# Reading the row of column numbers from PSUM in the one-hot matrices of a graph network's sum passes

## What is computed

```
h = relu(layernorm(x)); x = x + spline_conv(h, edge_attr)       # batch norm and ELU inside
h = relu(layernorm(x)); x = x + attention_conv(h)               # softmax over the edges of a node
h = relu(layernorm(x)); x = x + gcn3(h)
h = relu(layernorm(x)); x = x + sage(h)

gcn3:  three times  h = relu( sum over edges of (h @ W)[src] * norm  + self term + b )
sage:  concat(segment_sum(h[src], dst) / deg, h) @ W.T + b
segment_sum(src_rows, dst, num_segments=N)
```

## Time and profile before

| | |
|---|---|
| median of 3 runs | 13193.13 us (13179.23 to 13198.88) |
| profiled execution, time | 13194.91 us |
| profiled execution, span of the profile | 13193.0 us |
| PE busy | 7957.6 us (60%) |
| POOL busy | 8307.1 us (63%) |
| DVE busy | 5160.7 us (39%) |
| ACT busy | 1792.7 us (14%) |
| granted tensor clock, mean | 0.750 of full speed |

### The profile page before, as it was taken

The page is one execution under the profiler, slowest core; times in us unless marked ns, Lnnn a source line. Parts: engine busy times, 40 slices in busy tenths (PEclk is TensorE's granted clock), DMA queues, the critical chain, the costliest instruction groups (busy, mean ns, idle before and its releaser), DMA issues.

```text
span 13193.0 us, 199759 instructions
## 1 busy us (share of the span) xinstructions
PE 7957.6 (60%) x44286; PEld 5757.4 (44%) x44287; DVE 5160.7 (39%) x12670; ACT 1792.7 (14%) x4699; POOL 8307.1 (63%) x7522
## 2 busy tenths in 40 slices
PE   5878888888646666676666345534545345524445
PEld 5777888888534555555555111121112111101112
DVE  6545555555633333333334222232223222242223
ACT  0000011111123333333443000000000000000000
POOL 5788888777566666665442666646665566646664
PEclk9888899999767777788887566656666566656666
DMA  6111111111132222222221333323332232323332
GB/s 250 18 16 15 16 16 16 15 15 15 4 69 64 61 61 59 59 60 61 62 56 32 76 85 82 85 50 82 85 82 61 74 85 79 85 55 83 85 85 67
DMA packets 533179, 800.90 MB, mean 61 GB/s; under 512 B 319934, under 2 KB 329453, under 8 KB 532837
## 3 DMA queue, kind: packets, MB, share of 16 engines
q0 software_dynamic: 311952, 330.95, 14.0%
q1 hardware_dynamic: 218485, 466.48, 11.1%
q10 hardware_dynamic: 2400, 0.53, 0.0%
HBM read 700.08 MB, written 97.36 MB: 60 GB/s over the span
## 4 chain that ended last, share of the span: by engine, by line
issue 21%; DVEq 18%; PE 11%; another core or an unknown queue 10%; DVE 8%; ACT 3%; ACTq 1%; DMA 0%; POOL 0%; POOLq 0%; SPq 0%
DVEq L1329 4%; DVEq L1310 3%; DVE row_part L1310 3%; DVE R L1329 2%; DVEq L1325 2%; PE psAB L845 2%; PE psAB L851 2%; DVEq L357 2%; PE psCD L858 2%; DVEq L333 1%; DVEq L1305 1%; DVEq L1313 1%; DVEq L1309 1%; DVE A L1313 1%
## 5 line engine op out<-in xcount | busy, mean ns | idle before, releaser
L535 POOL DMA_INDIRECT gath<-sum_tab,idx_block x3584 | 3544.6, 989 | 2446.0 <-issue 1499.7
L885 PE MATMUL psAB<-gath,R 128*128 128x192 bf16 x4832 | 798.2, 308 | 3136.0 <-DVE R L1329 2351.8
L792 PE MATMUL psAB<-one_hot,R 128*128 128x128 f32 x15680 | 2322.2, 309 | 438.8 <-DVE one_hot L1105 322.5
L792 PEld LDWEIGHTS psAB<-one_hot,R 128*128 128x128 f32 x15680 | 2171.4, 214 | 482.8 <-issue 456.3
L535 POOL DMA_INDIRECT gath<-spline_tab,idx_block x1568 | 1984.8, 1266 | 615.4 <-issue 524.7
L535 POOL DMA_INDIRECT gath<-gat_tab,idx_block x1568 | 1524.0, 972 | 1336.2 <-DVEq L1038 897.6
L885 PEld LDWEIGHTS psAB<-gath,R 128*128 x4832 | 455.3, 102 | 3462.4 <-issue 3399.3
L1329 DVE SCALAR_TENSOR_TENSOR R<-iota_row,tile_base,dstf 128x512 f32 x1208 | 915.6, 758 | 2567.6 <-issue 2567.6
L511 POOL DMA_INDIRECT dense<-count_block,cell_block x672 | 1202.0, 1789 | 350.8 <-issue 187.4
L1134 DVE TENSOR_TENSOR R<-gath,R 128x2048 f32<-128x2048 f32 x392 | 900.2, 2297 | 413.0 <-DMA gath<-spline_tab,idx_block 398.1
L901 PE MATMUL psCD<-R,Q 128*128 128x512 f16 x1960 | 953.9, 487 | 42.1 <-issue 37.7
(11 more groups left out here) (251 smaller groups left out, 8922.3 us busy)
## 6 DMA issues: line engine op xcount, KB each, us to landing
R<-dense SPq DMA_DIRECT2D x280, 896.0 KB
Q<-dst_rows SPq DMA_DIRECT2D x392, 256.0 KB
dense<-stage SPq DMA_DIRECT2D x70, 896.0 KB
gath<-sum_tab,idx_block POOLq DMA_INDIRECT x3584
gath<-spline_tab,idx_block POOLq DMA_INDIRECT x1568
gath<-gat_tab,idx_block POOLq DMA_INDIRECT x1568
sum_tab<-Q SPq DMA_DIRECT2D x28, 672.0 KB, 5.5
dense<-count_block,cell_block POOLq DMA_INDIRECT x672
```

What stands on the lines that cost most here:

```text
L535: nc.gpsimd.indirect_dma_start(out=dest[:, s, j, :], out_offset=None, in_=table, in_offset=bass.IndirectOffsetOnAxis(ap=idx_block[:, c:c + ...
L792: nc.tensor.matmul(block, z[:, w, j, k * P:(k + 1) * P], oh32[:, j, :], start=(j == 0), stop=(j == J - 1))
L885: ins = nc.tensor.matmul(psAB[:, ring(v, 0, SV, 512, 3 * F)], oh16[:, bass.ds((v & (SV - 1)) * GE + j * P, P)], gath_sum[:, s, j, :], star ...
```

## The change

The sum passes' one-hot instruction reads the column numbers from columns 512 to 639 of `psE`, where each pass first copies them. A semaphore `iota_moved` with a register count orders the copy before the first read; the wait on `loaded_edges` beside it has been satisfied since the start. The spline pass's own one-hots (L1105) still read `iota_row`.

```diff
@@ tensors
         psE = pb("psE", 1024)
+        iota_sum = psE[:, 512:512 + P]
@@ semaphores
+        iota_moved = sem("iota_moved")
@@ vector engine
-            (folded,) = registers(dve, "dve_folded", 1)
+            folded, iotas = registers(dve, "dve_folded", 2)
             dve.reg_mov(folded, 1)
@@ sum_groups
                         V.scalar_tensor_tensor(oh16[:, ring(v, 0, SV, GE)].rearrange("p (j n) -> p j n", j=J),
-                                               iota_row[:, :].unsqueeze(1).to_broadcast([P, J, P]),
+                                               iota_sum.unsqueeze(1).to_broadcast([P, J, P]),
                                                tile_base[:, bass.ds(t, 1)],
                                                dstf[:, bass.ds(col, J)].unsqueeze(2).to_broadcast([P, J, P]),
                                                ALU.add, ALU.is_equal).then_inc(oh16_ready, 1)
@@ sum_pass
                 for r in then:
                     dve.reg_mov(r, 0)
+                V.tensor_copy(iota_sum, iota_row[:, :]).then_inc(iota_moved, 1)
+                dve.reg_add(iotas, iotas, 1)
+                dve.wait_ge(loaded_edges, 16 * 9)
+                dve.wait_ge(iota_moved, iotas)
+                V.engine_nop()
                 with dve.Fori(first, SI) as i:
                     sum_groups(i)
```

## The result

The change makes the kernel **slower by 0.4%**: 13254.5 us (median of 10 runs, 13237.9 to 13289.3) against 13205.2 us (10 runs, 13179.2 to 13212.9), ratio 1.0041, 95% interval 1.0031 to 1.0051. The forecast was 13080 us in a range of 13010 to 13205; the time lies above it, and on the side of rival B.

A forecast was written before the change was run, and what follows sets the result against it. A sum pass was taken to last as long as POOL's gathers plus its waits for DVE's slots. Of 161.3 us of hold-ups, 113 would be saved, added steps costing nothing: 13194.9 - 113 = 13082, forecast 13080 us, range 13010 to 13205.

The forecast's parts named there:

- rival B: Sum passes: steadier POOL stream slows DVE's queue sooner, so the change is slower, 13265 us at F = 7.0; chance 0.16.
- (1): Sum-pass gathers on POOL: hold-ups by L1329, all 161.3 us of excess over 944 ns each, disappear.
- (2): L1329 on DVE: reading PSUM leaves its 752 ns unchanged, bounds -75 to +86 us over 1208 instructions.
- (3): Start of each sum pass: the copy into psE, its wait and steps cost nothing, at most about 8 us.
- (4): Rounds of the sum passes: of the 161.3 us, 77 to 149 us are saved, middle taken, 113 us.
- F: Part of a 25.3 us sum-pass round in which DVE is quick: 9.0 us, assumed to shrink by 0 to 0.74 us.
- The mark named for B: Sign of rival B in the sum passes: clearly more than 218 waits of POOL.
- the forecast's wait: POOL's wait for DVE's slot per round of the sum passes, 853.7 / 218 = 3.9 us, assumed to stay.
- rival A's second half: Sum passes: POOL only waits longer, because DVE's slot comes at the same moment as before.
- Rival A: Sum passes: no gain, 13193 us within 26, as hold-ups stay or POOL only waits longer; chance 0.18.
- Its other half: Sum-pass gathers: the hold-up stays, since L1329 still reads dstf and the pointer scalar tile_base in SBUF.

The follow-up runs named there:

- copy_only: The changed kernel with the one-hot instruction reading iota_row in SBUF again, copy, wait and register steps kept; ratio 1.0001 to the kernel before.
- drag pair: drag_sbuf and drag_psum, both with DVE summing 2816 extra PSUM elements before each fold, one-hots from SBUF or PSUM; 13144.1 and 13115.0 us.
- brake: The changed kernel with POOL writing 64 columns of an unused tile after each group of four gathers, run twice; ratios 0.9908 and 0.9918.
- shorter code: DVE's 40 written-out groups as a loop of five over eight: kernel before, ratios 0.9992, 0.9996, 0.9988; changed kernel, 0.9892.
- shorter lead: The changed kernel with POOL at most two groups ahead instead of four in the sum passes; ratio 0.9897, against 0.9889 for the change there.
- before_2: The kernel before, unchanged, traced again in the surroundings of the experiments; 11359.9 us in a single execution.
- drag_sbuf: copy_only with DVE summing 2816 elements from PSUM into an unused column before each fold; 13144.1 us, ratio 1.1571 to the kernel before.
- drag_psum: The changed kernel with DVE summing 2816 elements from PSUM into an unused column before each fold; 13115.0 us, ratio 1.1543 to the kernel before.

## Why the prediction was wrong

**(1) The hold-ups: right.** 161.3 us were forecast to leave POOL's gathers, 158.1 us did, and none takes over 997 ns any longer.

**(2) The price of L1329: right.** 750 ns with PSUM in the median, 752 forecast. By the Trainium skill's figures for a PSUM source ("VectorE: DVE Perf Modes", on the TRN2 errata) it would be an estimated 65 ns longer. The runs decide against that: it is 8 ns shorter in the mean, and the multiply of L1134 is 7 ns shorter.

**(3) The added copy: right in the quick surroundings,** by copy_only; not tested in the first surroundings.

**(4) How much of it stays: wrong, and this decided the result.** I let the quick part F of a round shrink by 0 to 0.74 us, the hold-up of a round; no row gave its size, and I took the middle of two guesses. The measured rounds, counted by waits as I had done: 5592.6 / 301 = 18.6 us with 896 / 301 = 2.98 groups and a wait of 1110.0 / 301 = 3.7 us. By the same equation F / 2.8 + (18.6 - F) / 18 = 2.98, so F is 6.5 us, 2.5 less than the 9.0 of before. That is past the 1.4 us from which I had put rival B. The mark named for B, clearly more than 218 waits, is there: 301. So step (4) failed in the term F.

That B's price agrees is partly luck. At F = 7.0 it gave 6.24 us per group, 72 us more, 13265 us; measured were 6.24 us per group (5592.6 / 896), 70 us more in the windows, 13254 us in all. But with F at 6.5 and the forecast's wait of 3.9 us the equation gives some 6.3 us per group, about 150 us more; the shorter wait and a POOL group of 5.00 us make up the rest. And since F was worked out from the equation, it can't confirm it.

The kept traces allow a count without the equation. Call a register or branch step of DVE's queue of over 0.5 us slow, and a run of three or more, less than 4 us apart, a slow stretch. Before has 197 slow stretches in the four passes, after 228, so the 218 and 301 waits were not one to a round, as my sum had it. The quick part between two of them fell from 11.4 us to 9.7 in the mean, and the slow part from 16.5 to 14.7. In total the quick parts stayed (2203 and 2169 us), the slow parts grew (3247 to 3347), and the number of slow steps hardly moved: 2271 before, 2292 after. So the rounds became shorter and more, at the same number of slow steps. With looser or tighter bounds for a stretch the quick total still moves by less than 3%, and the slow total never falls by over 1%: neither pays back the 158 us.

What is shown and what is not: that the waits rose by more than the gathers lost is in the trace. That slow steps come on sooner is too: from POOL's last restart to the first slow step pass 7.9 us before and 6.4 after (medians of the stretches), and in both a stretch ends some 2 us after POOL has stopped. That it is the steadier stream which brings them on is argued. The drag pair fits it from the other side: a DVE slow on its own gives no loss and hardly more waits. But the brake, the shorter code and the shorter lead, which would have told, never met a slow queue. Nor is the cause of the 0.7 us steps known. The nearly equal number of them fits as well that a pass has its own total, with POOL's waits only filling what is left (rival A's second half), and some 50 us from elsewhere; no run decides between the two.

**Rival A** named the right cover (POOL only waits longer), and it describes most of what happened: 158 us saved in gathers went into 256 us more of waits. Its other half, that the pointer scalar keeps the hold-up, is refuted. The Trainium skill's rule ("SBUF — State Buffer", on the shared port pair) agrees with the gathers of the sum passes in all runs, up to 1.47 us or more with the row in SBUF and 1.02 us at most with it in PSUM, if a pointer scalar isn't counted as an input. For the other direction it doesn't fit: by the rule the loser waits for the whole instruction of the other, but beside gathers of 944 ns no one-hot of the sum passes took over 0.93 us (before_2), 0.18 us more than the shortest, and drag_sbuf lost only 29 us in all.

**The deeper error** was to price the step on one trace whose bound, a slow instruction queue, I could not explain, and to give its unexplained behaviour only 0.16.

## What to carry to other kernels

A DVE instruction that reads two SBUF tensors held up POOL's gathers for the rest of its run, less about 0.1 us; placing one small repeated operand in PSUM cost nothing per instruction here (750 against 752 ns, 2287 against 2294) and, where gathers set the pace, saved the hold-ups (1.1% here, 5.8% with the spline's multiply). Look first at whether the engine that gains is the one that is waited for: with DVE as the bound the same step gave 0.2%, and with a DVE queue that turns slow it cost 0.4%. When register steps of one kind have two durations, find what switches them before pricing anything that changes the rhythm around them.

## What was not expected of the hardware

- The same kernel took 13205 us and 11363 us in two surroundings. The sum passes differ by 890 us (5522 and 4632), and the visible difference there is the queue steps, at most 0.14 us in one and up to 1.4 us in the other (L357 on DVE).
- The slow steps come in stretches while POOL streams gathers: some 6 to 8 us after it restarts, and gone some 2 us after it stops. Their number hardly changed when the stream did (2271 and 2292).
- The hold-up works both ways. A gather that starts during L1329 waits for its rest; L1329 in turn took 769 ns in the mean in drag_sbuf, 750 in drag_psum, 22 us over 1208 instructions.
- In the spline pass the multiply of 2.3 us stretched gathers of 0.95 us to as much as 3.1 us, the longest gather of before_2:

```profile
L535 POOL DMA_INDIRECT gath<-spline_tab,idx_block x1568: 940/947/3087, 129.5 to 3338.6; - x196
```
